# An attention and mixture-of-experts layer on one core: work of the last two batches moved behind the first max transpose, identity turns in two holes, stores held

## The reference

```python
xn = layernorm(x)                                  # x: 8 batches x 512 tokens x 128
# attention, 16 heads of 8; rope here is one factor per batch and feature
q, k, v = rope(xn @ Wq.T), rope(xn @ Wk.T), xn @ Wv.T
att = softmax(q @ k.T / sqrt(8)) @ v
# mixture of experts: 32 experts of 64, 6 chosen in 4 of 8 groups
scores = sigmoid(xn @ gate_w.T)
combine = normalised scores of the 6 chosen * 2.5  # tokens x experts
moe = sum_e relu(xn @ up_e.T)**2 * combine[:, e] @ down_e.T
shared = relu(xn @ shared_up.T)**2 @ shared_down.T
out = x + att + moe + shared
```

## Time and profile before

| | |
|---|---|
| median of 3 runs | 703.16 us (708.97, 697.25, 703.16) |
| profiled execution, its own time | 697.23 us |
| its span | 695.4 us |
| TensorE granted clock, mean of the span | 0.974 |
| PE / DVE / POOL / ACT busy | 97% / 70% / 59% / 58% |

### The profile page before, as it was taken

How to read it: one execution, slowest core, us unless ns; L and a number is a source line. 1 busy time by engine, 2 the same in 40 slices (tenths; PEclk the granted TensorE clock), 3 DMA queues, 4 the chain that set the end, 5 groups by cost and what they waited for, 6 DMA issues and landing times. The chain is left out here.

```text
span 695.4 us, 11331 instructions
## 1 busy us (share of the span) xinstructions
PE 672.9 (97%) x3902; PEld 343.3 (49%) x3902; DVE 486.5 (70%) x1114; ACT 401.5 (58%) x771; POOL 411.7 (59%) x344
## 2 busy tenths in 40 slices
PE   6897999999999999999999999999999999999996
PEld 5342355445554454555555454555544555445443
DVE  6585668678776878678776968678766968676500
ACT  2453356665566555665656656665656656665662
POOL 5691246665675557565676557564766556566555
PEclk9896599999999999999999999999999999999999
DMA  7838032543463343533463343542463343332210
GB/s 202 257 73 243 6 92 65 184 95 90 123 193 87 91 109 96 186 95 71 123 213 81 77 118 103 188 99 57 115 213 96 72 114 92 95 93 64 72 22 15
DMA packets 53224, 77.84 MB, mean 112 GB/s; under 512 B 5296, under 2 KB 19504, under 8 KB 53040
## 3 DMA queue, kind: packets, MB, share of 16 engines
q1 hardware_dynamic: 51440, 75.56, 40.9%
q10 hardware_dynamic: 1728, 1.57, 0.9%
HBM read 57.19 MB, written 19.40 MB: 110 GB/s over the span
## 5 line engine op out<-in xcount | busy, mean ns | idle before, releaser
L628 DVE TENSOR_REDUCE nmax<-sc 128x1 f32<-128x512 f32 x512 | 330.8, 686 | 157.0 <-PE sc L792 155.0
L453 ACT ACTIVATE probs<-st 128x512 f32<-128x512 f32 x512 | 278.9, 595 | 243.2 <-PE st L802 234.8
L338 POOL TENSOR_TENSOR gated<-gate_at,relu 128x512 f32<-128x512 f32 x128 | 162.9, 1273 | 245.0 <-ACT relu L458 244.8
L792 PE MATMUL sc<-stacks 33*128 33x512 f32 x512 | 204.0, 469 | 6.3 <-DVE nmax L628 3.3
L802 PE MATMUL st<-stacks 35*128 35x512 f32 x512 | 191.2, 454 | 1.7 <-DMA stacks<-m_parts 1.7
L802 PEld LDWEIGHTS st<-stacks 35*128 35x128 f32 x512 | 78.6, 187 | 208.8 <-issue 104.4
L342 POOL TENSOR_TENSOR g<-gated,relu 128x512 f32<-128x512 f32 x128 | 163.2, 1275 | 18.6 <-PE acc L819 0.5
L819 PE MATMUL acc<-dn,g 128*128 128x128 f32 x1024 | 139.3, 279 | 1.4 <-POOL g L342 1.4
L813 PE MATMUL pv<-probs,v_aug 128*32 128x512 f32 x1024 | 138.1, 612 | 0.0
L819 PEld LDWEIGHTS acc<-dn,g 128*128 128x128 f32 x1024 | 126.5, 193 | 16.7 <-issue 13.5
L837 PE MATMUL upb<-xnT,up 128*128 128x512 f32 x256 | 133.5, 604 | 0.0
(11 more groups left out here) (102 smaller groups left out, 397.2 us busy)
## 6 DMA issues: line engine op xcount, KB each, us to landing
gate_at<-gate_rows SPq DMA_DIRECT2D x64, 512.0 KB, 6.7
q_stack<-qk_parts SPq DMA_DIRECT2D x32, 256.0 KB, 6.5
stacks<-q_stack SPq DMA_DIRECT2D x64, 128.0 KB, 2.5
stacks<-k_stack SPq DMA_DIRECT2D x64, 128.0 KB, 2.7
k_stack<-qk_parts SPq DMA_DIRECT2D x28, 256.0 KB, 5.7
gate_at<-in_x SPq DMA_DIRECT2D x8, 256.0 KB, 5.0
x_res<-in_x SPq DMA_DIRECT2D x8, 256.0 KB, 3.2
out<-y SPq DMA_DIRECT2D x8, 256.0 KB, 2.2
```

What stands on the lines that cost most here:

```text
L338: nc.gpsimd.tensor_tensor(gated[:, u % 2, :], gate_at[:, group % RING, u % GATES, :], relu[:, u % RELUS, :], ALU.mult).then_inc(gated_read ...
L453: nc.scalar.activation(probs[:, u % 2, h, :], st_b[h % 2][:], ACT.Exp).then_inc(probs_ready, 1)
L628: nc.vector.tensor_reduce(out=nmax[:, s % 2, at:at + 1], in_=sc_b[i % 2][:], op=ALU.max, axis=AXX, negate=True).then_inc(s_read, 1)
L792: nc.tensor.matmul(sc_b[i % 2][:], stacks[rows, s % NQ, 0, pr, qt * P:(qt + 1) * P], stacks[rows, s % NQ, 1, pr, :], start=True, stop=True ...
```

## The change

PRELUDE: 36 identity turns in place of 20 ahead of `("x", 1)`, and 20 new ones after `("k", 2)`. BESIDE loses x, q and k of batches 6 and 7 and the last logits; they form a new list BEHIND, one item behind each of the eight score tiles that follow `max_transpose(0)`. ACT does `load_max(0)` between the two lists. `("v", 0)` stands before `("x", 5)`, and the gate transpose waits for 6 batches of xnT in place of 8. The turn of batch 6 waits until ACT has copied the maxima out of `tr`. On SP, `store_parts(1)` waits until the max rows of step 0 have landed.

```diff
-        PRELUDE = [("warm", 32), ("x", 0), ("warm", 6), ("q", 0), ("k", 0), ("logits", 0), ("warm", 20), ("x", 1),
-                   ("warm", 6), ("q", 1), ("k", 1), ("x", 2), ("x", 3), ("q", 2), ("k", 2), ("std", 2), ("sig", 0)]
-        BESIDE = [("q", 3), ("k", 3), ("logits", 1), ("x", 4), ("logits_out", 1), ("q", 4), ("k", 4), ("x", 5),
-                  ("v", 0), ("q", 5), ("k", 5), ("shared", 0), ("x", 6), ("shared", 1), ("q", 6), ("k", 6),
-                  ("x", 7), ("gate", 0), ("q", 7), ("k", 7), ("logits", 2), ("logits_out", 2)]
+        PRELUDE = [("warm", 32), ("x", 0), ("warm", 6), ("q", 0), ("k", 0), ("logits", 0), ("warm", 36), ("x", 1),
+                   ("warm", 6), ("q", 1), ("k", 1), ("x", 2), ("x", 3), ("q", 2), ("k", 2), ("warm", 20),
+                   ("std", 2), ("sig", 0)]
+        BESIDE = [("q", 3), ("k", 3), ("logits", 1), ("x", 4), ("logits_out", 1), ("q", 4), ("k", 4), ("v", 0),
+                  ("x", 5), ("shared", 0), ("q", 5), ("shared", 1), ("k", 5), ("gate", 0)]
+
+        BEHIND = [("x", 6), ("q", 6), ("k", 6), ("x", 7), ("logits", 2), ("q", 7), ("k", 7), ("logits_out", 2)]
@@ sync
             load_gates(0)
+            sp.wait_ge(m_ld[0], MAXES * 16)
             store_parts(1)
@@ scalar
-            for kind, i in PRELUDE + BESIDE:
+            for kind, i in PRELUDE + BESIDE + [("max", 0)] + BEHIND:
...
+                elif kind == "max":
+                    load_max(0)
...
-            load_max(0)
@@ tensor, transpose_x
+                if i == 6:
+                    pe.wait_ge(m_ready, 1)
@@ tensor, prelude
                 elif kind == "gate":
-                    pe.wait_ge(xnT_ready, B)
+                    pe.wait_ge(xnT_ready, 6)
@@ tensor
             max_transpose(0)
             for i in range(FIRST_AHEAD):
                 score(TILES + i)
+                for kind, n in BEHIND[i * len(BEHIND) // FIRST_AHEAD:(i + 1) * len(BEHIND) // FIRST_AHEAD]:
+                    prelude(kind, n)
```

## The result

The changed kernel takes 707.59 us (median of 10 runs, 703.87 to 708.37) against 698.07 for the kernel before (10 runs, 695.82 to 708.97): ratio **1.0128**, 95% interval 1.0096 to 1.0159. The profiled execution took 707.78 us, 10.55 more than that of before.

A forecast was written before the change was run, and what follows sets the result against it. PE, busy 97% of the span, was taken as the bound, with gains only ahead of some 94 us. 697.23 - 0.7 (earlier start) - 1.0 (part of unit 0 at full clock) = 695.5 us; range 682 to 706.

The forecast's parts named there:

- in most executions the clock falls there: Pause of PE ahead of unit 0, near 62: clock falls about 5 us later than before; forecast's chance 0.42.
- rival B: Clock falls in the hole of ACT's DMA issues, moved work up to +6.0: 702.5 us, up to 708 median; chance 0.13.
- the prediction's own sum: Ahead of the max transpose: without 7.4 us of items PE alone gets there at 45.8, DVE allows only 49.5.
- The max transpose at 49.83 (forecast 49.5): Max transpose, paced by DVE's row maxima with routing pieces: expected at 49.5, bounds 47 and 51.
- Rival A: Clock stays up throughout: -0.7, -2.8 in unit 0, -8.8 in units 1 to 3, giving 684.9 us; chance 0.35.
- rival C: Added prelude turns don't hold the clock; 27.70 to 34.50 stays at 1.2 GHz, DVE 2.7 us later: 698.2; chance 0.06.
- The moved work from its first projection to the last sigmoid: Behind the max transpose: first projection at 52.7, items to 61.1, turn back and sigmoid to 62.4.
- ACT's DMA issues on the path: After the max transpose: two issues, 1.9 us together, hold up batch 6's copy and so the first moved projection.
- The table load directly ahead of the first exponential: ACT ahead of unit 0: the 1.28 us load, formerly hidden, is now on the path; first exponential 63.7.
- The steady part: From unit 4 on: units follow at 4.7 us and the change touches nothing there.
- The rows landed by 58.00 (forecast 58.4): Max rows with SP's stores held: land by 58.4, before PE reaches unit 0 at 62.4; earns nothing by itself.
- The scatter: Slower runs of the kernel before: guessed to spend more time at 1.2 GHz, some of it removed by filled holes.

The follow-up runs named there:

- Run 3: Changed kernel with 12 more identity turns in PE's pause ahead of the max transpose; 703.75 us, ratio 1.0093 to the kernel before.
- runs 4: Also `fill_both`: changed kernel plus 12 turns ahead of the max transpose and 12 behind the second score tile after it; 700.25 us, ratio 1.0022.
- 5: Changed kernel plus 12 turns ahead of the max transpose, 12 in the hole behind it, 6 ahead of unit 0, and 10, 3, 3 in units 0 and 1; 697.05 us.
- 11: The kernel of run 10 with about a quarter to a third fewer turns; 692.23 us, ratio 0.9892 to the kernel before.
- run 6: Changed kernel with turns in every pause up to unit 1, also behind score tiles 10 to 12 and ahead of the second max transpose; 691.61 us, ratio 0.9914.
- run 1: The kernel before with the 36 and 20 identity turns alone, nothing moved or held; 696.52 us, ratio 0.997.
- `turns_held`: The kernel before with the 36 and 20 turns and the held stores, without the moved work; 694.03 us, ratio 0.9944.
- run 8: `turns_held` plus 3 turns behind each of the eight score tiles and 8, 3, 3 and 12 in units 0 and 1; 689.79 us, ratio 0.9897.
- `before`: The kernel before the change, with the old prelude; 698.07 us, median of 10 runs.
- `behind_only`: The changed kernel with the old PRELUDE and without the held stores, so the moved work alone; 708.83 us, ratio 1.0144 to the kernel before.
- `held_only`: The kernel before with the held stores alone, one new wait on SP; 704.15 us, ratio 0.9964, as a time inconclusive.
- run 10: The kernel of run 6 with ACT's max-row DMA issues behind the copy of batch 6, and 3 turns for 12 in that hole; 690.39 us, ratio 0.9895.
- run 7: The kernel before with the held stores alone (`held_only`, ratio 0.9964) and with the 36 and 20 turns too (`turns_held`, ratio 0.9944).

## Why the prediction was wrong

The forecast was 695.5 us, within 2% of before; measured are 707.59.

**The step that failed is the forecast's own**: "in most executions the clock falls there", at the pause ahead of unit 0. It fell some 11 us earlier, at 50.5. The prediction had a fall near 50 under rival B with 0.13, and put it at another cause: the hole made by ACT's DMA issues, which ends at 53.02, where PE has waited 0.67 us for ACT. The fall came before that hole. Ahead of it was the wait for DVE's cut, 1.3 us, and a stretch in which PE waited for DVE again and again. Run 3 fits both: with the first pause filled, the clock fell at ACT's hole, 3.6 us later. But in runs 4, 5 and 11 it fell at 43 to 44, in the stretch with the waits for DVE, ahead of either. What is shown (run 6) is that with the pauses from 38 to 54 and those in and ahead of units 0 and 1 all filled, the clock stays up; which of them makes it fall is not settled.

**How that pause came about was in the prediction's own sum, unread.** It found that PE alone would reach the max transpose at 45.8 and DVE only at 49.5. Those 3.7 us are PE's idle time (3.3 were measured, 2.0 and 1.3), and the moved items were what had filled them: before, PE was busy for 14.00 of 14.00 us. Of the 7.4 us of items, the max transpose came only 4.4 us earlier for it (49.83 against 54.25 in run 1, or 3.7 against 53.50 in `turns_held`). The other 3 to 4 us had run beside DVE for nothing, and behind the max transpose all of them are on the path. The max transpose at 49.83 (forecast 49.5) is right; the price of being early was not drawn.

**Rival B's size.** It gave 702.5 on the profiled execution, +6.0 in the moved work. There it was 71.37 - 63.7 = 7.7. That its "up to 708 in the median" lies so near 707.59 is luck: it came from adding the scatter of before, and the changed kernel hardly scatters (703.87 to 708.37). Missing altogether was that the low clock then lasts longer: the relu of unit 3 is 10.4 us late, 7.0 of it at the first exponential, and 3.9 in units 1 to 3 (26.76 us in place of 22.90), less 0.4 in unit 0. The gap before unit 3 is 9.57 us against 6.44: before, the clock had come back by then.

**Rival A's size.** 684.9 rested on 4.7 us a unit at the full clock. Units 1 to 3 take 18.7 (run 8). The error could be seen before: the gap from 87.73 to 94.17 is 6.44 us and at the clock 1.00 (the row shown with run 8). An average of 14 later units was set against three that are longer at the same clock; what makes them longer is not shown.

**What was right.** The turns hold the clock (rival C falls: 1.00 from 27.00 to 34.50, with 20 turns and then score tiles ahead of it). All eleven kernels with the 36 and 20 turns have it up there in their traces; of the three with the old prelude two fall (`before`, `behind_only`) and one does not (`held_only`), so the prize of these turns is smaller than rows 2 alone made it look. The moved work from its first projection to the last sigmoid: 9.7 us forecast, 10.0 at the full clock (56.73 to 66.70, run 6). ACT's DMA issues on the path: 1.3 us by run 10, of 1.9. The table load directly ahead of the first exponential: 70.08 and 71.37. The steady part did not move: from the relu of unit 3 to the end of the span are 601.2 us before and 601.4 after. The rows landed by 58.00 (forecast 58.4), far ahead of the first product at 70.16, so the held stores are off the path in the changed kernel, though no run of it without them alone was made. That they would earn 3.4 of the 4.1 us with the moved work left where it was (run 7) was not seen.

**The scatter.** That the slower runs of before had more time at 1.2 GHz was a guess. The 11 to 28 runs of it beside each experiment bear it out in the main: 694.6 us at a mean granted clock of 0.979, 704.4 at 0.964. Three executions of before stand outside of that (750.51 us at 0.831, 1500.47 and 2064.6 at 1.0); no trace shows what they did.

## What to carry to other kernels

Before work is moved off an engine's stretch, ask who sets the pace there. If another engine does, part of the work was free where it stood (3 to 4 of 7.4 us here), and taking it away leaves a pause that may cost the clock as well. Here the clock was at half for 51 us behind a stretch with waits of 0.3 to 1.3 us on TensorE. Filling the longest wait alone gave back little (ratio 1.0093 in place of 1.0128); identity turns in every pause kept the full clock (0.9914).

When a sum ends in "engine A would be there at 45.8, engine B at 49.5", the difference is a term of its own. And a unit's cost at the full clock is to be read from that unit, in a stretch at the full clock, not from an average of later ones.

## What the runs showed of the hardware

**Identity turns held the clock.** With turns in all pauses it stayed at 1.00 to the end (run 6, run 8). In `fill_both` it came back from 0.50 at 53.6, while 12 turns ran (51.38 to 53.84). At the start the pace of the turns rose from 5.0 to 9.5 per us, though the granted clock prints as 1.00 for both the earlier trace rows. The rule of the Trainium skill, "TensorE: Matmul & The Clock Gate" (Part 4: PE-mode transpose), that transpose mode doesn't count as PE-busy in the same way, does not fit these turns, which the trace lists as MATMUL.

**Once low, the clock did not come back though PE was nearly always busy**: 12.31 of 13.00 us and 20.98 of 22.80 at 0.50 in the changed kernel. In `fill_both` PE was busy for 9.00 of 9.00 us from 44.00 to 53.00, at 0.50 all the way. No single kind of work marks the return: it came at 34.5 in the prelude and in unit 2 in the kernel before, in unit 3 in the changed one, at 71 in the moved work of `behind_only`, and in identity turns in `fill_both`. What decides it is open.

**Waits for a small DMA behind large ones.** In run 1 the product waited until 63.31 for two DMAs of 8 KB issued at 55.23, beside eight stores issued from 52.98 to 59.62. With the stores held, SP's wait shows when the rows had landed, since the stores start then: at 58.00 in the changed kernel and at 58.41 in `turns_held`. The changed kernel first, then `turns_held`:

```profile
50.82 1.45 SPq L249 DMA_DIRECT2D gate_at<-gate_rows  x2
58.00 2.73 SPq L227 DMA_DIRECT2D q_stack<-qk_parts  x4
```

```profile
50.87 1.33 SPq L247 DMA_DIRECT2D gate_at<-gate_rows  x2
58.41 2.49 SPq L225 DMA_DIRECT2D q_stack<-qk_parts  x4
```

The rows were issued at 50.43 and at 54.48, so they took 7.6 and 3.9 us; from the issue of the two gate loads (512 KB each) they took 7.2 and 7.5 us. The busy share of the DMA engines falls to 0.00 from 58 to 59 in both. So even with the stores out of the way the rows landed when those loads were through. That they waited for them is not proved, as no run held the gate loads back.
